# The experts' first layer of a vision tower with its two matmul operands exchanged, one GELU for 768 columns, and transposes on the matmul engine

## The reference

```python
logits = xn2 @ w_gate                       # 8 experts
top_vals, top_idx = jax.lax.top_k(logits, 2)
gates = jax.nn.softmax(top_vals, axis=-1)
...
h = jax.nn.gelu(xn2 @ w1 + bb1, approximate=False)    # w1: 192 x 768
return (acc + g[:, None] * (h @ w2 + bb2), None)      # w2: 768 x 192
```

## Time and profile before

| | us |
|---|---|
| median of 3 runs | 1188.52 (1186.59 to 1189.37) |
| the profiled execution, its time | 1187.29 |
| its span in the trace | 1185.5 |
| mean granted TensorE clock | 0.935 of full speed |
| PE busy | 999.9 (84%) |
| PEld busy | 860.4 (73%) |
| DVE busy | 678.8 (57%) |
| ACT busy | 452.6 (38%) |
| POOL busy | 545.3 (46%) |

### The profile page before, as it was taken

How to read it: one execution, slowest core, us unless ns; L and a number is a source line. 1 busy time by engine, 2 the same in 40 slices (tenths; PEclk the granted TensorE clock), 3 DMA queues, 4 the chain that set the end, 5 groups by cost and what they waited for, 6 DMA issues and landing times.

```text
span 1185.5 us, 23992 instructions
## 1 busy us (share of the span) xinstructions
PE 999.9 (84%) x6992; PEld 860.4 (73%) x6993; DVE 678.8 (57%) x1791; ACT 452.6 (38%) x1140; POOL 545.3 (46%) x1047
## 2 busy tenths in 40 slices
PE   6969999999997987489888888888629999999960
PEld 4768899889875654377767777677518999999960
DVE  5465576585436788646788878888532222222216
ACT  1233233324113444323555555555204434343424
POOL 1385677586521222213566666666512333343430
PEclk9989999999988998789999999999659999999995
DMA  8447562561102400302600000000011111111118
GB/s 347 165 173 303 219 243 93 215 268 64 37 11 53 68 1 0 56 1 86 268 16 15 15 15 15 15 15 19 21 50 34 43 41 44 37 42 41 44 33 252
DMA packets 41701, 103.09 MB, mean 87 GB/s; under 512 B 7046, under 2 KB 28656, under 8 KB 38837
## 3 DMA queue, kind: packets, MB, share of 16 engines
q1 hardware_dynamic: 30085, 88.86, 21.6%
q0 software_dynamic: 5760, 9.68, 2.4%
q10 hardware_dynamic: 5808, 3.96, 1.1%
HBM read 86.30 MB, written 18.32 MB: 88 GB/s over the span
## 4 chain that ended last, share of the span: by engine, by line
PE 44%; issue 17%; POOLq 13%; DVE 10%; POOL 7%; DMA 4%; DVEq 2%; ACT 2%; SPq 1%; ACTq 0%
PE pe L1602 15%; PE pp L967 5%; PE pe L951 4%; PE pe L1611 3%; POOLq L559 3%; POOLq L537 2%; PE pe L954 2%; POOLq L526 2%; DMA x<-yy_d 2%; POOL xs_d L529 1%; POOL xn L532 1%; POOL hall L540 1%; POOLq L510 1%; DVE sc L316 1%; PE pe L183 1%
## 5 line engine op out<-in xcount | busy, mean ns | idle before, releaser
L1602 PE MATMUL pe<-wm,xm 128*128 128x193 f32 x1008 | 174.2, 332 | 1.2 <-DVEq L1406 1.2
L1602 PEld LDWEIGHTS pe<-wm,xm 128*128 128x128 f32 x1008 | 168.4, 193 | 5.6 <-issue 4.0
L834 ACT ACTIVATE hT<-pe,eb 128x128 f32<-128x128 f32 x336 | 92.7, 375 | 147.5 <-PE pe L954 147.5
L967 PE MATMUL pp<-w2s,hT 128*128 x672 | 118.5, 327 | 0.0
L967 PEld LDWEIGHTS pp<-w2s,hT 128*128 128x128 f32 x672 | 107.9, 191 | 0.2
L951 PE MATMUL pe<-xsT,ew 128*128 128x128 f32 x672 | 90.1, 286 | 3.5 <-ACT xsT L824 3.5
L756 DVE TENSOR_TENSOR ys<-pp,b2s 128x192 f32<-128x192 f32 x56 | 20.0, 358 | 124.8 <-PE pp L967 124.8
L951 PEld LDWEIGHTS pe<-xsT,ew 128*128 128x128 f32 x672 | 81.7, 197 | 8.7 <-ACT xsT L824 4.1
L555 POOL DMA_INDIRECT yy_d<-ys,yix x56 | 65.4, 1168 | 46.4 <-issue 46.4
L529 POOL DMA_INDIRECT xs_d<-xsrc,dst x64 | 65.4, 1022 | 41.6 <-issue 41.6
L1331 POOL TENSOR_TENSOR sqs<-sqs,sqt 128x448 f32<-128x448 f32 x56 | 67.9, 1212 | 8.0
(11 more groups left out here) (273 smaller groups left out, 2316.1 us busy)
## 6 DMA issues: line engine op xcount, KB each, us to landing
xm<-in_xm SPq DMA_DIRECT2D x7, 2688.0 KB, 15.2
raw<-in_xwa SPq DMA_DIRECT2D x7, 1792.0 KB, 7.5
raw<-in_xwb SPq DMA_DIRECT2D x7, 1536.0 KB, 10.9
x<-in_x SPq DMA_DIRECT2D x4, 1536.0 KB, 8.9
xs<-xs_d SPq DMA_DIRECT2D x56, 96.5 KB
x<-yy_d SPq DMA_DIRECT2D x8, 672.0 KB
w1s<-in_W SPq DMA_DIRECT2D x1, 4608.0 KB
w2s<-in_W SPq DMA_DIRECT2D x1, 4608.0 KB
```

Source lines behind the costliest of these rows:

```text
L834: last = f(self.hT[:, u, c], pe1[:, 2 * u + c % 2, (c // 2) * ROWS:(c // 2 + 1) * ROWS], ACT.Gelu, bias=self.b1[:, u, c:c + 1])
L967: last = mm(pp[:, u, 0:D], self.hT[:, u, n], self.w2s[:, bass.ds(e, 1), n * D:(n + 1) * D].rearrange("p o d -> p (o d)"), start=(n == 0), ...
L1602: mm(y[:, 0:D + 1], cell(q, c), wm[:, q, c], start=(q + c == 0), stop=(q == 3 and c == KC - 1))
```

## The change

The first layer's operands are exchanged: the transposed tokens `xsT` are stationary and the weights move, in two halves of HH = 384 hidden units. The full-row products read `w1s` directly; only the 64-row part, whose two halves stand in one table of 384 columns, is still copied by DVE, to `wr`. The hidden layer then has tokens on partitions, so its bias is a row: a table of 8 x 768 values is loaded into all 128 partitions, in the place of `x2`, and DVE adds it from PSUM into `hid`. ACT applies GELU to 768 columns in one instruction, in place. PE transposes the result in six pieces into the other two banks of `pe1`, and DVE copies 768 columns to `hT`. The pipeline is one slot deeper, the second layer moves from `item(3)` to `item(4)`. Host side, the weights are laid out to fit; the numbers computed are the same.

```diff
@@ vector: expert(item)
+            if (z := item(1)):
+                i, u, h = z
+                e = dve.value_load(self.meta[0:1, 0, bass.ds(i, 1)], min_val=0, max_val=E - 1)
+                wait(dve, self.e_h, i - 1)
+                v.tensor_copy(self.wr[:, u], self.w1s[:, bass.ds(e, 1), HID:W1C].rearrange("p o f -> p (o f)")).then_inc(self.e_wc, 1)
-            if (a := item(1)):
+            if (a := item(2)):
                 i, u, h = a
                 e = dve.value_load(self.meta[0:1, 0, bass.ds(i, 1)], min_val=0, max_val=E - 1)
-                dve.wait_ge(self.e_g, 2 * i + 2)
-                v.tensor_copy(self.b1[:, u], self.b1s[:, bass.ds(e, 1), :].rearrange("p o c -> p (o c)"))
-                v.tensor_copy(self.w1[:, u], self.w1s[:, bass.ds(e, 1), :].rearrange("p o f -> p (o f)"))
-                dve.drain().then_inc(self.e_wc, 1)
-            if (c := item(3)):
+                dve.wait_ge(self.e_h, i + 1)
+                wait(dve, self.h_T, i - 1)
+                v.tensor_tensor(self.hid[:, u].rearrange("p (c f) -> p c f", c=2), pe1[:, 0:2, 0:HH],
+                                self.b1s[:, bass.ds(e, 1), :].rearrange("p o (c f) -> p (o c) f", c=2), ALU.add).then_inc(self.h_add, 1)
+            if (b := item(3)):
+                i, u, h = b
+                dve.wait_ge(self.h_T, i + 1)
+                wait(dve, self.e_y, i - 1)
+                v.tensor_copy(self.hT[:, u].rearrange("p c n -> p (c n)"), pe1[:, 2:4].rearrange("p a n -> p (a n)")[:, 0:HID]).then_inc(self.h_out, 1)
+            if (c := item(4)):
@@ scalar
-            act.wait_ge(self.e_wc, i + 1)
-            act.wait_ge(self.y_free, i + 1)
-            act.wait_ge(self.e_h, i + 1)
-            for c in range(HC):
-                last = f(self.hT[:, u, c], pe1[:, 2 * u + c % 2, (c // 2) * ROWS:(c // 2 + 1) * ROWS], ACT.Gelu, bias=self.b1[:, u, c:c + 1])
-                if c % 3 == 2:
-                    last.then_inc(self.e_g, 1)
+            act.wait_ge(self.h_add, i + 1)
+            f(self.hid[:, u], self.hid[:, u], ACT.Gelu).then_inc(self.e_g, 1)
         def both(item):
+            expert(item)
             hidden(item)
-            expert(item)
@@ tensor: expert(item)
+                e = pe.value_load(self.meta[0:1, 0, bass.ds(i, 1)], min_val=0, max_val=E - 1)
                 pe.wait_ge(self.e_xT, i + 1)
+                wait(pe, self.h_add, i)
+                for c in range(2):
+                    mm(pe1[:, c, 0:HH], self.xsT[:, c], self.w1s[:, bass.ds(e, 1), c * HH:(c + 1) * HH].rearrange("p o f -> p (o f)"), start=True, stop=False, skip_group_check=True)
                 pe.wait_ge(self.e_wc, i + 1)
-                for n in range(HC):
-                    mm(chunk(n), self.w1[:, u, n * P:(n + 1) * P], self.xsT[:, n % 2], start=(n < 2), stop=False, skip_group_check=True)
-                for n in range(HC):
-                    r = slice(LOW, P) if n % 2 == 0 else slice(0, LOW)
-                    last = mm(chunk(n), self.w1[r, u, HID + (n // 2) * P:HID + (n // 2 + 1) * P], self.xsT[r, 1 - n % 2], start=False, stop=True, skip_group_check=True)
+                for c, r in ((0, slice(LOW, P)), (1, slice(0, LOW))):
+                    last = mm(pe1[:, c, 0:HH], self.xsT[r, 1 - c], self.wr[r, u], start=False, stop=True, skip_group_check=True)
                 last.then_inc(self.e_h, 1)
...
+            if (d := item(3)):
+                i, u, h = d
+                pe.wait_ge(self.e_g, i + 1)
+                wait(pe, self.h_out, i)
+                for n in range(HC):
+                    last = T_(pe1[:, 2 + n // 4, (n % 4) * P:(n % 4 + 1) * P], self.hid[:, u, n * P:(n + 1) * P], ident)
+                last.then_inc(self.h_T, 1)
-            if (c := item(3)):
+            if (c := item(4)):
                 i, u, h = c
                 e = pe.value_load(self.meta[0:1, 0, bass.ds(i, 1)], min_val=0, max_val=E - 1)
-                pe.wait_ge(self.e_g, 2 * i + 6)
+                pe.wait_ge(self.h_out, i + 1)
@@ load of the bias rows (sync)
-                         (self.b1s[:], A["b1"].rearrange("e p c -> p e c")),
+        sp.wait_ge(self.c_x, NP)
+        sp.wait_ge(self.res_set, NP)
+        sp.dma_start(self.b1s.rearrange("p e f -> p (e f)"), A["b1"].rearrange("e f -> (e f)").unsqueeze(0).to_broadcast([P, E * HID])).then_inc(self.b1_ld, 16)
         sp.wait_ge(self.meta_set, 1)
```

More of the change, by code:

```diff
@@ L57 @@
 LOW = D - P
-W1C = HID + HID // 2
+HH = HID // 2
+W1C = HID + HH
 ROWS = 128
@@ L87, with wait @@
 NCONST = C_SC + 2
+def wait(eng, sem, count):
+    if not (isinstance(count, int) and count <= 0):
+        eng.wait_ge(sem, count)
 def run_slots(eng, n, depth, slot, unroll=2, start=0, stop=None):
@@ L379, in __init__ @@
         own = ExitStack()
-        self.w1 = sb("ew1", [P, 2, W1C], to=own)
-        self.b1 = sb("eb1", [P, 2, HC], to=own)
+        self.wr = sb("ewr", [P, 2, HH], to=own)
+        self.hid = sb("hid", [P, 2, HID], to=own)
         self.xs = sb("xs", [P, 2, DX], to=own)
@@ L427, in __init__ @@
         self.yix = sb("yix", [P, 2], I32)
+        self.b1s = x2[:].rearrange("p i d -> p (i d)").rearrange("p (e f) -> p e f", e=E)
         self.yl = x2[:].rearrange("p (a i k) d -> p a i k d", a=4, i=4)
@@ L441, in __init__ @@
         self.ew_ld, self.e_wc, self.y2_set = sem("ew_ld"), sem("e_wc"), sem("y2_set")
+        self.h_add, self.h_T, self.h_out, self.b1_ld = sem("h_add"), sem("h_T"), sem("h_out"), sem("b1_ld")
         self.e_st = [sem("e_st0"), sem("e_st1")]
@@ L546, in expert @@
         def expert(item):
-            if (a := item(4)):
+            if (a := item(5)):
                 i, u, h = a
@@ L563, in gpsimd @@
         pool.wait_ge(self.dum_set, 1)
-        run_slots(pool, NT, 5, expert)
+        run_slots(pool, NT, 6, expert)
     def clear(self, dve):
@@ L591, in vector @@
         dve.drain().then_inc(self.y_free, 2)
-        dve.drain().then_inc(self.e_g, 4)
         dve.drain().then_inc(self.xs_used, 2)
@@ L738, in vector @@
         v.memset(self.xdum[:], 0.0).then_inc(self.dum_set, 1)
[L741 removed]
+        dve.wait_ge(self.ew_ld, 16 * 3)
+        dve.wait_ge(self.b1_ld, 16)
         def expert(item):
[L744 removed]
+            if (z := item(1)):
[4 more added lines that the diff above has]
+            if (a := item(2)):
                 i, u, h = a
                 e = dve.value_load(self.meta[0:1, 0, bass.ds(i, 1)], min_val=0, max_val=E - 1)
[L747 to L751 removed]
+                dve.wait_ge(self.e_h, i + 1)
[8 more added lines that the diff above has]
+            if (c := item(4)):
                 i, u, h = c
@@ L757, in expert @@
                 dve.drain().then_inc(self.y_free, 1)
-        run_slots(dve, NT, 5, expert)
+        run_slots(dve, NT, 6, expert)
         dve.wait_ge(self.res_set, NP)
@@ L829, in hidden @@
             i, u, h = b
-            act.wait_ge(self.e_wc, i + 1)
-            act.wait_ge(self.y_free, i + 1)
-            act.wait_ge(self.e_h, i + 1)
-            for c in range(HC):
-                last = f(self.hT[:, u, c], pe1[:, 2 * u + c % 2, (c // 2) * ROWS:(c // 2 + 1) * ROWS], ACT.Gelu, bias=self.b1[:, u, c:c + 1])
-                if c % 3 == 2:
-                    last.then_inc(self.e_g, 1)
+            act.wait_ge(self.h_add, i + 1)
+            f(self.hid[:, u], self.hid[:, u], ACT.Gelu).then_inc(self.e_g, 1)
         def both(item):
+            expert(item)
             hidden(item)
-            expert(item)
-        run_slots(act, NT, 5, both)
+        run_slots(act, NT, 6, both)
         for n in range(NP // 4):
@@ L968, in expert @@
                 last.then_inc(self.e_y, 1)
-        pe.wait_ge(self.ew_ld, 16 * 4)
-        run_slots(pe, NT, 5, expert)
+        pe.wait_ge(self.ew_ld, 16 * 3)
+        run_slots(pe, NT, 6, expert)
     def load_weights(self, sp):
@@ L1748, in lay_out @@
     g["wgate"] = halves(f["L0_ffn_w_gate"])
-    w1 = f["L0_ffn_W1"].reshape(E, D, HC // 2, 2, P)
-    wide = np.stack([w1[:, :P, :, 0], w1[:, LOW:, :, 1]], 3).reshape(E, P, HID)
-    rest = np.concatenate([w1[:, :LOW, :, 1], w1[:, P:, :, 0]], 1).reshape(E, P, HID // 2)
+    w1 = f["L0_ffn_W1"]
+    wide = np.concatenate([w1[:, :P, :HH], w1[:, LOW:, HH:]], 2)
+    rest = np.concatenate([w1[:, :LOW, HH:], w1[:, P:, :HH]], 1)
     g["W1"] = np.ascontiguousarray(np.concatenate([wide, rest], 2))
-    g["b1"] = np.ascontiguousarray(f["L0_ffn_b1"].reshape(E, HC, P).transpose(0, 2, 1))
+    g["b1"] = f["L0_ffn_b1"]
     g["W2"] = np.ascontiguousarray(f["L0_ffn_W2"].reshape(E, HC, P, D).transpose(0, 2, 1, 3))
```

6 lines of the change are left out of this document (1 added, 5 removed).

## The result

The changed kernel took 1218.46 us (median of 4, 1217.7 to 1223.96), the kernel before beside it 1188.94 us (median of 4). The ratio is 1.0257, 95% interval 1.0227 to 1.0288: slower, by 29.5 us. The profiled execution took 1219.07 us with a span of 1217.1 us, 31.8 more than the profiled one of before.

The account below looks back on a forecast made before the run. PE was taken to bound the kernel, 4.58 us a round. 54 rounds x 0.45 = 24.3, less 2.4 for the last round, plus 1.8 (fill) and 2.5 (bias load): 26.2 us more, 1215 us, range 1202 to 1240.

Parts of the forecast that it names:

- The pace: Expert stage: PE sets the round, 5.03 us against 4.58 before; chance 0.76 for 4.9 to 5.15 us.
- POOL at 4.2 to 4.5 us: Expert round of the kernel before: the nearest limit behind PE, holding the round there if PE were quicker.
- Full rows: First layer, full rows: two products of 384 columns, two passes each, take 1.30 us instead of 1.49.
- 64 rows: First layer's 64-row part: two products of 384 columns take 0.85 us, 0.33 each and 0.2 for steps.
- the two passes of one product run side by side: 64-row products on half the array: passes overlap, 0.33 us a product; rival without this 1232 to 1250 us, chance 0.09.
- GELU transposes: Before the second layer: six transposes of GELU's output add 0.66 us a round, none beside other PE work.
- DVE: DVE's expert round takes 4.4 us, under PE's 5.03, with register loads partly covered.
- The prediction's 5.7 us with no load covered: Rival: DVE bounds the expert round at 5.7 us if its register loads are never covered, 1251 us; chance 0.06.
- The hidden layer's single PSUM buffer: Between first layers: the addition ends about 1.4 us after the first layer, covered by 2.9 us of PE work.
- The start: Before the expert stage: the bias load delays a scatter by 2.5 us, between 0 and 7.6.
- The first product to the first second layer: Filling the expert stage's pipeline: 13.7 us instead of 11.95, 1.8 more.
- The rival by which eight transposes in a round would bring the clock down: Expert stage: clock falls to its lower level, round 9.9 us, kernel about 1480 us; chance 0.02.

Follow-up runs that it names:

- e2: The changed kernel with five of the six transposes of GELU's output left out in the hardware loop's slots; 1198.95 us, ratio 1.0043.
- e3: The kernel before with six transposes of the identity matrix added in front of each second layer; 1224.3 us, ratio 1.024.
- e4: The changed kernel with both 64-row products on the same half of the array's rows; 1264.96 us, ratio 1.0573.
- e8: The changed kernel with each 64-row product done twice, two on one half, then two on the other; 1257.41 us in one run.
- e6: The changed kernel with two unused DVE additions (1152 and 576 columns, between SBUF tiles) in every round; 1250.28 us, ratio 1.0438.
- e5: The changed kernel with one more unused DVE copy of 1152 columns between SBUF tiles in every round; 1227.81 us, ratio 1.0248.
- e10: The kernel before with an unused 3072 KB bias load at the changed kernel's point of SP's queue; 1200.35 us, ratio 1.0055.
- e7: The changed kernel with the bias load held back for ACT's row copies, released one copy too early; 1226.77 us, ratio 1.0248.
- e11: The changed kernel run once more, unaltered, on the chip of two other follow-up runs; 1230.51 us, ratio 1.0323.
- e1: The changed kernel with the bias load moved in SP's queue behind the wait for the last scatter; 1225.45 us, ratio 1.0257.
- e9: The changed kernel with the bias load held back until ACT has written the rows for the last scatter; 1219.03 us, ratio 1.0215.

## Why the prediction came out as it did

**The pace.** Right for the changed kernel. PE sets it, with no gap, and a round's added columns appear in full: 5.11 us against the predicted 5.03. e2 and e3 show it from both sides, by taking transposes away and by adding them to the old kernel. For the kernel before it was right but for 0.06 us: the nearest other limit was not POOL at 4.2 to 4.5 us but the loop over ACT, which set the 4.58, while PE's own passes are 4.53. The 1.49 us of the old full rows hold this wait beside the step to another kind of pass.

**Full rows: 1.38 us, predicted 1.30.** This is the term that was too small. The starts in this group are 0.323 us apart, as predicted, but the step from the last full pass (961.904) to the first 64-row pass (962.32) is 0.416. Such a longer step occurs three times around the 64-row group: at the way in, after its first pair (0.42) and at the way out (0.42). The prediction kept the last two, as the 0.2 us that it left in the 64-row group, and had said that the old 1.49 us hold a part of this kind, but left the first out of the new 1.30. 0.08 us a round is 4.3 us of the kernel.

**64 rows: 0.85 us as predicted, for another reason.** The step "the two passes of one product run side by side" failed (e4: 1.48 us on one half; e8: eight passes on two halves in 1.50). The halves overlap, each at its own pace. That the number came out is owed to equal work on the two halves. Both readings give half the serial time when the halves hold equal work, which is why could not tell them apart. They part when they don't: the prediction's reading would have put e4 at 0.85.

**GELU transposes: 0.66 us as predicted**, and the whole cost of the change in the round: 54 x 0.66 = 35.6 us, of which 54 x 0.13 = 7.0 come back in the first layer, about half of it from the wider products (0.07) and half because ACT's copy is no longer late (0.06).

**DVE.** Not the bound, as predicted; its own round is 3.6 us by e6 rather than 4.4. Only one of the three register loads stands bare: DVE is idle before the weight copy for 59.2 us in 52 rounds, 1.14 each, beside 2.56 us of work. The prediction's 5.7 us with no load covered does not follow from its 1.2 us a load, which make 6.1. The copy of 768 columns from PSUM takes 0.95 us where 0.91 was predicted. The Trainium skill ("VectorE: DVE Perf Modes", "Why PSUM operands drop a tier") has such a copy at one column a cycle; the trace agrees, since 0.76 us suffice for 1152 columns between SBUF tiles in e5.

**The hidden layer's single PSUM buffer.** No cost: PE never waits for the addition between 905 and 1170 us. The cover is thin, though: with 1.95 us more on DVE (e6) the addition is what PE waits for.

**The start.** The bias load was predicted at 2.5 us between bounds of 0 and 7.6, and cost 5.1 in the trace and 0.55% in e10. Place and victim were right. The size was not: the load runs 10.3 us instead of 7.6, 305 GB/s from issue to landing instead of the 415 of the earlier trace rows, and the scatter lands only when it does (7.48 us from 856.02 is 863.50; the load ends at 863.3). In the trace's packets the load lasts from 853.99 to 862.96, and those of the two scatters issued behind it run only from 859.0 to 863.1, among its last. The same holds in e2, e4, e5, e6, e7, e8, e10 and e11 and for the tile load in e1: the short transfer lands 0.1 to 0.3 us behind the load. By that rule a load of 7.6 us would have cost 2.4 us, an estimate from these rows, so the term was mis-sized by the load's length. The first product to the first second layer takes 12.7 us, 0.8 more than before and not 1.8.

**The clock.** The rival by which eight transposes in a round would bring the clock down did not occur: the granted clock was 1.00 from 905 to 1170 us, and in every other run from 950 to 1100. The Trainium skill (the same TensorE page, Part 4) has it that transposes don't count for the clock gate; with 0.93 us of transposes in 5.11 us of unbroken PE work no effect is seen, and no run here has more of them.

**Sum.** The 26.2 us become 31.8 in the profiled pair: 4.3 from the kind change, 2.6 from the load, 1.8 that had come before the load was issued; against it 1.7 less at the end, and 1.4 less in the fill and the last rounds. The 1.8 us are not the change's: they go with the granted clock of that execution, as shown under e11. Against the medians (29.5) the forecast was 3 us short.

**A version that beats both** did not come out. With one transpose of six left the round is 4.57 us (e2) against 4.58, so even with the transposes nearly gone the new first layer gains nothing. Without the last one it would be 4.46, an estimate by the same step of 0.109 us: 54 x 0.12 = 6 us, about what the bias table costs at the start where the changed kernel loads it. The best form of the change found is e9, at 1.0215.

## What to carry to other kernels

When an engine is busy without a gap, price an exchange by its passes: turning the operands round saves a little in the steps between narrow passes (0.07 us here) and costs every transpose that the turned output needs (0.66). But a PE busy all the time can still wait a little: look whether a round's first weight load follows at once on another engine's last work (0.05 us behind ACT's copy here). In these runs a bulk load cost a short transfer behind it the rest of the load, so it belongs where only compute is on the path and the short transfers that matter are ahead of it. And when one row fits two mechanisms, ask in which order of work they would differ, before building a term on one.

## What the runs showed of the hardware that I had not expected

- 64-row fp32 passes of 384 columns: 0.32 us a pass on one half, two halves at once in pairs 6 to 13 ns apart, and no cost for writing all of one half first (1.50 us for eight passes so ordered, 1.48 for four on one half).
- Between passes of 384 columns over 128 rows and over 64 rows the step is about 0.09 us longer: at the way in, once more behind the first pass of the new kind, and at the way out to the token transposes (0.416, 0.42 and 0.42 against 0.323).
- A scatter of 2.3 us takes 7.2 to 9.2 us when a load of 3072 KB was issued 1.5 to 3 us ahead of it, on another queue, and lands 0.1 to 0.3 us behind it; the load itself takes 10.0 to 11.6 us.
- In the kernel before, PE was busy for all of 219.59 us and yet waited about 0.06 us a round for ACT's copy: the weight load started 0.05 us behind it, and the round's second pass 0.17 us behind the first instead of 0.11.
